# Causal attention with row maxima: diagonal tiles copied by ScalarE, masked by a GpSimd select and reduced from SBUF, in place of mask matmuls

## The reference, cut to what matters

```
att = jnp.einsum('bhqd,bhkd->bhqk', q, k) * scale
att = att + alibi[None]
att = att + causal[None, None]          # -inf above the diagonal
att = jax.nn.softmax(att.astype(jnp.float32), axis=-1)
y = jnp.einsum('bhqk,bhkd->bhqd', att, v)
```

## Time and profile before

| | |
|---|---|
| Time, three runs | 551.94, 554.82, 554.70 us; median 554.7 us |
| The profiled execution | 557.83 us, of which the span of the trace is 556.1 us |
| Busy: PE, DVE, ACT, POOL | 514.5, 298.9, 229.1, 177.5 us |
| Projections with unit 0's row maxima | to 50.7 us |
| Steps 0 to 7 | 57.8 to 274.8 us |
| The rest (output projection, routing, experts, norms) | 274.8 us to the end |

### The profile page before, as it was taken

How to read it: one execution, slowest core, us unless ns; L and a number is a source line. 1 busy time by engine, 2 the same in 40 slices (tenths; PEclk the granted TensorE clock), 3 DMA queues, 4 the chain that set the end, 5 groups by cost and what they waited for, 6 DMA issues and landing times.

```text
span 556.1 us, 7466 instructions
## 1 busy us (share of the span) xinstructions
PE 514.5 (93%) x2538; PEld 256.4 (46%) x2538; DVE 298.9 (54%) x624; ACT 229.1 (41%) x465; POOL 177.5 (32%) x247
## 2 busy tenths in 40 slices
PE   5987999999999999988889899989999999999991
PEld 2432333333333333321166655555656666566661
DVE  1789888888888888860075451211213333334241
ACT  3441676767676767678601131101112222322220
POOL 4432223322222222222100109730022554545543
PEclk9999999999999999999977989999999999999997
DMA  7772455545453545071328100320121221222210
GB/s 225 134 194 73 78 170 89 159 89 175 86 180 87 179 82 183 20 239 47 101 66 285 44 0 1 132 76 20 57 85 49 66 76 59 68 76 57 66 48 28
DMA packets 36868, 54.92 MB, mean 99 GB/s; under 512 B 5647, under 2 KB 24931, under 8 KB 36724
## 3 DMA queue, kind: packets, MB, share of 16 engines
q1 hardware_dynamic: 29792, 30.96, 21.3%
q0 software_dynamic: 7040, 23.50, 13.5%
HBM read 34.76 MB, written 17.52 MB: 94 GB/s over the span
## 4 chain that ended last, share of the span: by engine, by line
PE 81%; DVE 10%; ACT 4%; issue 2%; DMA 1%; POOL 1%; POOLq 0%; SPq 0%; ACTq 0%; DVEq 0%
PE ps L728 14%; PE ps L548 11%; PE ps L523 10%; PE ps L648 10%; PE ps L537 9%; DVE mx L879 7%; PE ps L747 7%; PE ps L659 5%; PE ps L493 3%; PE ps L620 3%; PE ps L739 2%; ACT probs L807 2%; PE ps L525 2%; PE ps L637 1%; PE ps L610 1%
## 5 line engine op out<-in xcount | busy, mean ns | idle before, releaser
L879 DVE TENSOR_REDUCE mx<-ps 128x1 f32<-128x512 f32 (+4 forms) x312 | 183.0, 643 | 29.0 <-PE ps L525 20.9
L807 ACT ACTIVATE probs<-ps 128x512 f32<-128x512 f32 x288 | 151.1, 606 | 68.6 <-PE ps L537 68.6
L523 PE MATMUL ps<-qk_or_dn 127*128 127x512 bf16 (+3 forms) x384 | 117.4, 331 | 5.5 <-DVE mx L879 3.9
L537 PE MATMUL ps<-qk_or_dn 127*128 127x512 bf16 x288 | 100.5, 380 | 2.9 <-ACT probs L807 2.6
L1155 POOL TENSOR_SCALAR_AFFINE_SELECT probs<-probs 128x512 f32<-128x512 f32 x64 | 40.5, 633 | 164.5 <-ACT probs L807 164.5
L728 PE MATMUL ps<-wgu,tmp 128*128 x184 | 82.9, 593 | 0.1
L548 PE MATMUL ps<-probs,Vs 128*32 128x512 f32 x576 | 76.7, 605 | 0.7 <-ACT probs L807 0.7
L523 PEld LDWEIGHTS ps<-qk_or_dn 127*128 127x128 bf16 x384 | 37.1, 97 | 80.1 <-DVE mx L879 63.7
L1203 POOL DMA_INDIRECT rows<-acc,tok x23 | 22.7, 986 | 89.9 <-DMA acc<-x_all 45.1
L1068 DVE TENSOR_TENSOR tmp<-tmp,ps 128x512 f32<-128x512 f32 x23 | 15.8, 688 | 65.0 <-PE ps L728 65.0
L525 PE MATMUL ps<-cb 128*128 128x128 bf16 x256 | 50.6, 222 | 0.0
(11 more groups left out here) (121 smaller groups left out, 470.9 us busy)
## 6 DMA issues: line engine op xcount, KB each, us to landing
wgu<-in_gu POOLq DMA_DIRECT2D x8, 1024.0 KB, 6.1
qk_or_dn<-qparts SPq DMA_DIRECT2D x36, 128.0 KB
yT<-yU SPq DMA_DIRECT2D x16, 256.0 KB, 2.1
qk_or_dn<-in_dn SPq DMA_DIRECT2D x8, 512.0 KB, 8.0
tmp<-xs SPq DMA_DIRECT2D x23, 128.5 KB
qparts<-wgu SPq DMA_DIRECT2D x6, 384.0 KB, 3.3
tmp<-yT SPq DMA_DIRECT2D x34, 64.0 KB
xs<-rows POOLq DMA_DIRECT2D x1, 2056.0 KB, 10.2
```

The costliest lines, as they stand in the source:

```text
L523: mm = pe.matmul(o, q, K6[k][0:KROWS, k0:k0 + w], start=True, stop=not masked)
L537: pe.matmul(o, K6[k][0:KROWS, kb * P:(kb + 1) * P], Q6[k][0:KROWS, :, qi * P:(qi + 1) * P], start=True, stop=True).then_inc(s_st, 1)
L807: act.activation(probs[:, 4 * (s % 3) + p, :], ps[:, 4 + (4 * s + p) % SB, :], ACT.Exp, scale=SCALE).then_inc(s_exp, 1)
L879: dve.tensor_reduce(o, ps[:, a_bank(u, t), 0:nh * w].rearrange("p (h w) -> p h w", h=nh), AX.X, ALU.max).then_inc(s_amax, 1)
```

## The change

A unit's row-max tiles are cut anew. The diagonal block of each `qi` is a tile of its own: 4 heads of 128 keys in one bank, 8 such tiles for a unit. What lies beside the diagonal makes 30 tiles. The mask matmuls and their constant are gone. A diagonal tile goes another way: ACT copies the bank to SBUF (`copy_diag`, two buffers `dg`), POOL fills the part above the diagonal with -3e38 (`cut_diag`), and DVE reduces it from SBUF, four places later in the stream than its own place (`BEHIND`). Its bank is freed by ACT's copy. A unit has 39 places now.

The parts of `split_max` are laid between the first four reductions of the next stream, with one more maximum (`join_max`) ahead of them; the transposition stands at place 6 instead of 3. Each step takes the stream 20 places ahead instead of 15, 14 places run before step 0, step 0 takes 45 and step 6 takes 20. The maxima of a unit are written with one transfer instead of three. POOL's later loads are issued one group later in a step.

```diff
 def row_max_tiles():
-    tiles = []
+    beside = []
+    for qi in range(1, NQ):
+        w = min(qi, 4) * P
+        per = 4 * P // w if w != 3 * P else 1
+        beside += [(qi, h, per, 0, w, LEFT) for h in range(0, HG, per)]
+        if qi > 4:
+            w = (qi - 4) * P
+            per = 4 * P // w if w != 3 * P else 1
+            beside += [(qi, h, per, 4 * P, w, RIGHT) for h in range(0, HG, per)]
+    tiles, n = [], len(beside) - 1
     for qi in range(NQ):
-        w = min(qi + 1, 4) * P
...
+        tiles.append((qi, 0, HG, qi * P, P, DIAG))
+        tiles += beside[n * qi // NQ:n * (qi + 1) // NQ]
+    return tiles + beside[n:]
...
+LEAD, AHEAD, FIRST_AHEAD = 6, 20, 14
+BEHIND, ND = 4, 2
+SPLITS = 4
-LEAD, AHEAD = 3, 15
-ORDER = (SHORT, LONG) * 4 + (SHORT,)
+ORDER = (SHORT, LONG) * 4 + ("SMSMSMWS",)
+def unit_tiles(u):
+
+    tiles = max_stream(u + 1)[AHEAD if u else FIRST_AHEAD:] if u + 1 < NU else []
+    return tiles + (max_stream(u + 2)[:AHEAD] if u + 2 < NU else [])
+def unit_order(u):
+    return (LONG,) * GROUPS if u == 0 else ORDER
+def reduce_order(u):
+
+    own, late = max_stream(u), []
+    out = []
+    for at, (v, t) in enumerate(own):
+        if is_diag(t):
+            late.append((at + BEHIND, (v, t)))
+        else:
+            out.append((v, t))
+        while late and late[0][0] <= at:
+            out.append(late.pop(0)[1])
+    assert not late
+    return out
...
-                for p in range(3):
-                    sp.dma_start(Q6[i][p:p + 1, :, :].rearrange("o h t -> o (h t)")
-                                 .rearrange("o (a b) -> o a b", a=n),
-                                 mrow[p * n:(p + 1) * n, :]).then_inc(s_mrow, 16)
+                sp.dma_start(Q6[i][0:M_ROWS, :, :].rearrange("p h t -> p (h t)")
+                             .rearrange("p (a b) -> p a b", a=HG * NQ), mrow[:]).then_inc(s_mrow, 16)
...
                 if i >= 3:
-                    pe.wait_ge(s_amax, i - 2)
+                    beside, diag = freed(i - 3)
+                    if FREED_BY_ACT[i - 3]:
+                        pe.wait_ge(s_dcopy, diag)
+                    else:
+                        pe.wait_ge(s_amax, beside)
...
-                    masked = diag < w
-                    mm = pe.matmul(o, q, K6[k][0:KROWS, k0:k0 + w], start=True, stop=not masked)
-                    if masked:
-                        mm = pe.matmul(o[:, diag:diag + P], id16, mask_qk, start=False, stop=True)
+                    mm = pe.matmul(ps[:, bank, i * w:(i + 1) * w], Q6[k][0:KROWS, h0 + i, qi * P:(qi + 1) * P],
+                                   K6[k][0:KROWS, k0:k0 + w], start=True, stop=True)
...
+            def copy_diag(u, t, bank):
+
+                n = NQ * u + A_TILES[t][0]
+                act.wait_ge(s_aps, max_index(u, t) + 1)
+                if n >= ND:
+                    act.wait_ge(s_dmax, n - (ND - 1))
+                act.activation(dg[A_TILES[t][0] % ND], ps[:, bank, :], ACT.Copy).then_inc(s_dcopy, 1)
...
-                qi, h0, nh, k0, w, second = A_TILES[t]
+                qi, h0, nh, k0, w, kind = A_TILES[t]
+                if kind == DIAG:
+                    dve.wait_ge(s_dcut, NQ * u + qi + 1)
+                    dve.tensor_reduce(mxd[:, :, qi], dg[qi % ND].rearrange("p (h w) -> p h w", h=HG), AX.X, ALU.max
+                                      ).then_inc(s_dmax, 1)
+                    return
...
+            def join_max(u):
+
+                dve.wait_ge(s_amax, freed(max_index(u, NA - 2))[0])
+                dve.tensor_tensor(mx0[:, :, 5:NQ], mx0[:, :, 5:NQ], mx1[:], ALU.max).then_inc(s_split, 1)
+                dve.wait_ge(s_split, u * 5 + 1)
+                dve.wait_ge(s_dmax, (u + 1) * NQ)
+                dve.tensor_tensor(mxs, mx0[:], mxd, ALU.max).then_inc(s_split, 1)
...
+            def cut_diag(u, t):
+
+                n = NQ * u + A_TILES[t][0]
+                pool.wait_ge(s_dcopy, n + 1)
+                tile = dg[n % ND].rearrange("p (h w) -> p h w", h=HG)
+                pool.affine_select(tile, tile, [[0, HG], [-1, P]], ALU.is_ge, least, base=0, channel_multiplier=1
+                                   ).then_inc(s_dcut, 1)
```

186 lines of the change are left out of this document (114 added, 72 removed).

## The result

The changed kernel takes 558.9 us (median of 10 executions, 556.1 to 560.7), the kernel before 554.6 us (10 executions, 551.9 to 555.5). The ratio of the executions is 1.009 with a 95% interval of 1.007 to 1.011 (the two medians alone would give 1.008): slower, and outside the forecast range of 540.5 to 551.0. The profiled execution took 559.95 us, its span is 558.2.

What follows compares the result with a forecast made beforehand. PE's queue was taken to bound steps 1 to 5, DVE the start. Terms +1.0 (through step 0), -9.7 (steps 1-5), -1.3 (step 6) sum to -10.0 us: 544.7 from median 554.7, stated as 545.0, range 540.5 to 551.0.

Steps and rivals of the forecast that it cites:

- I take +1.5 us (0 to +3): Start, beside the projections: late diagonal reductions make DVE wait for PE's tiles at about four of eight job boundaries; +1.5 us.
- first scores at +0.3: First scores after the start: transposition waits for three more reductions, about 1.5 us, the single transfer returns 1.2; +0.3 us.
- Step 0 itself, -0.8: Step 0: 45 places instead of 40 but no 32 masks, 9.2 us of work instead of 10.1; -0.8 us taken.
- The transposition now comes earlier, so I cost this at nothing: Single transfer of a unit's maxima: lands before the next unit's first score, covered by a full group; no cost.
- 26.0 us a step: Steps 1 to 5: PE's floor of 25.83 us plus 0.2 for waits, instead of 27.94; -9.7 us over five steps.
- the 1.84 written: Steps 1 to 5: 32 mask matmuls of a unit leave PE's queue at 0.0575 us each; -1.84 us a step.
- I take -1.3 us: Step 6: 16 masks (-0.9) and six places go, groups run at ACT's pace, the unspread split is two operations longer; -1.3 us.
- DVE as the bound: Rival, chance 0.16: late diagonal tiles and full banks add 1 us to DVE's 24.0, step 27.0 us, time 550.
- The slower rival: Rival, chance 0.08: DVE waits for each diagonal tile, eight a step; 0.7 us each gives 562, 1.0 about 572.
- ACT's copies against scores: Rival "nothing gained", chance 0.08: copies between exponentials delay PE by 0.23 us each, cancelling 1.84 us; 553 to 556.
- The clock rival: Rival, chance 0.06: the low clock lies over step 0's first groups, 3.5 us at half speed, up to 3 us; 548.
- The port between DVE and POOL: Rival, chance 0.04: selects hold back four two-operand SBUF operations at a unit's boundary, up to 0.63 us each; 547.5.

Runs made afterwards that it cites:

- e5: Changed kernel without the detour: DVE reduces diagonal tiles straight from PSUM, no ACT copies, POOL selects or causal mask in the row maxima; ratio to before 0.992.
- e6: Changed kernel with ACT's copies of unit 0's diagonal tiles ahead of the next job's first copy; ratio to the kernel before 1.006.
- e8: Changed kernel with the edits of e1, e6 and e7 together, and POOL's loads at groups 4 and 7 (4 and 8 in step 0); ratio to before 0.996.
- e9: e8 with the expert slots cleared at the end of step 6 (s == 8) instead of s == 4; 546.8 us, ratio to the kernel before 0.985.
- e10: e8 with the last transposition back in the change's place, slots cleared at s == 4; ratio to the kernel before 0.990.
- e13: e9 with the slots cleared at the start of step 6 (s == 1); median 546.1 us against 554.6 before, ratio 0.984.
- e7: Changed kernel with the last unit's transposition six places later in step 6; ratio to the kernel before 1.014.
- e12: Changed kernel with e7's late transposition, e8's loads and e9's clearing, the start left as the change has it; ratio to before 0.999.
- e2: Changed kernel with POOL's second load of a step one group later (groups 4 and 7 instead of 4 and 6); ratio to the kernel before 1.004.
- e3: Changed kernel with three transfers for the maxima, as before the change; ratio to the kernel before 1.012.
- e11: Kernel before with the second 1 MB load of a step moved to its maxima's transfer (s == 7 instead of 5); ratio to before 1.020.
- e4: Kernel before without its mask matmuls, row maxima over the whole diagonal block; ratio to before 0.987, a step 26.86 us.
- e1: Changed kernel with DVE's reductions beside the projections dealt out by job, never asking for the next job's tile; ratio to before 1.006.

## Why the prediction was wrong

**"I take +1.5 us (0 to +3)" for the start.** This step failed most. Up to the end of step 0 the forecast was +1.0 us and +11.1 came: +6.7 at unit 0's last reduction, where +1.5 was taken, +0.5 to the first scores and +3.9 in step 0. It counted what DVE's queue loses by asking for a tile of the next job, and never laid ACT's queue beside it. There the copy that frees PE's bank stands behind up to three operations of a projection job, one of which waits for DVE. The runs show it: without the detour the maxima of unit 0 come 4.2 to 6.8 us earlier (e5); moving the copies halves DVE's waits for PE (e6); both edits of order bring them from 58.7 to 62.2 us down to 55.0 to 56.0 (e8, e9, e10, e13).

The same code also varied: unit 0's maxima came at 61.4, 62.2 and 61.3 us (after, e7, e12) and at 58.9 and 58.7 (e2, e3). The traces show where most of that arises. A window within the ring and DVE's longest wait for PE near it, first of the changed kernel, then of e2:
```profile
30.00:36.00 6.00, 4.38 (x13) 1.90 (x13) 1.75 (x3) 2.11 (x4) 2.35 (x3) 0.72 0.72 176
36.44 0.69 DVE L958 TENSOR_REDUCE mx<-ps 128x1 f32<-128x512 f32 x1 [3.11 <-PE ps L575]
```
```profile
30.00:36.00 6.00, 3.98 (x19) 1.66 (x20) 3.29 (x6) 2.07 (x5) 1.59 (x3) 1.00 0.77 211
34.00 0.69 DVE L958 TENSOR_REDUCE mx<-ps 128x1 f32<-128x512 f32 x1 [1.42 <-PE ps L575]
```
Where the clock falls to 1.2 GHz inside the ring (a projection's matmul takes 1.16 us at 32.20 and took 0.59 at 24.71), the same wait is 3.1 us and not 1.4. e7 has it at the same place, e12 between 44 and 53 us (0.62 granted, a wait of 3.09 us); in e2 and e3 the clock stays at 1.00 up to 53 us. That is 1.7 of the 2.5 us between after and e2; the other 0.8 stand there already at DVE's first reduction that waits for PE (22.50 for 21.74). So a part of the miss at the start is a low clock in the changed kernel's profile that the prediction did not have either.

The next step, first scores at +0.3, was right at its core: the maxima are copied 4.1 us behind the last reduction instead of 2.6, and from the first issue to the first score it is 3.4 us instead of 4.4, so the single transfer gives 1.0 back and not 1.2 (first scores at 65.00, 57.81 before: +7.2, of which 6.7 were there at the last reduction). Step 0 itself, -0.8, was wrong by 4.7 us: from the first scores to its end it takes 34.25 us where 30.31 did before. The low clock (2.1 us) and the wait for the maxima of unit 1, behind the load of 88.54 (1.3 us), make 3.4 of them; the rest isn't placed. In e8, e12 and e13, which don't have that wait and have the low clock some 3 us long there, it takes 32.2 us.

**"The transposition now comes earlier, so I cost this at nothing. Its cover is a full group."** Cover against what came 1.8 us after the issue. I named PE's work behind the transfer and not the queue ahead of it: the diff moves POOL's loads from groups 3 and 5 to 4 and 6, and a 1 MB load ahead of a 24 KB transfer makes 3.3 us into 6.2. e2 (taken away), e3 (number of transfers ruled out) and e11 (made in the kernel before) show it from three sides. The 1.8 us were also the wrong row for the single transfer, which takes 3.3 us with nothing ahead of it. In steps 1 to 5 it is worth 0.5 us each (26.58 to 26.08).

**"26.0 us a step", -9.7.** Right in size once the loads are moved: 26.04 to 26.24 in e2, e8 to e10, e12 and e13. The terms under it were half right. The masks alone give 1.08 us and not the 1.84 written, since DVE at 23.8 us then delays the transposition (e4). The other 0.8 us came with the new stream, the spread split and the detour, where the prediction had the transposition's 0.42 less 0.15 for the finer tiles; which of them gives how much isn't shown, but without the detour the step stays at 26.5 (e5). The floor "25.83" was a tenth or two too low. DVE busy 23.75, ACT 23.50 and POOL 14.36 are the forecast 24.0, 23.6 and 14.0.

**Step 6, "I take -1.3 us": +1.7.** The split in a row was put at two small operations, some 0.4 us. PE stood 3.15 us instead of 1.2: DVE still had 1.15 us of reductions when PE had nothing more to do, where before a weighing of 1.07 us stood, and the split took 0.8 us more and not 0.4. Two of its operations took 0.40 and 0.50 us instead of 0.17 and 0.18, the second inside a select of POOL (245.48 to 246.16). The low clock behind the hole took about another 0.5 us: e1 and e3 have the same hole of 3.15 us, a full clock behind it, and 27.66 and 27.54 us for the step (with 1.2 and 1.0 us of waiting for the last maxima in it), where the changed kernel has 28.14. The true room was larger than forecast, too: with the transposition late and the transfer free, step 6 takes 23.63 us, 2.8 less than before (e9, e12, e13). I had the room at 1.3 because I counted the groups' pace and left the hole of before in.

**The rivals.** DVE as the bound: no; in steps 1 to 5 it waited for PE and never for a select. The slower rival placed the loss at DVE's wait for a diagonal tile; the sign was its, the mechanism wasn't. ACT's copies against scores cost nothing in the steps, where only 1.9 us of PE's waits in five steps were for maxima and 0.6 for `kparts` (Q and K's load, also costed at nothing). The clock rival came true in part: the low clock lay over step 0's first groups at the price it named (2.1 us where it said up to 3), on top of the rest. It isn't the detour's alone, since e5 and e13 have it from 50 to 61 us too, where DVE is the bound. It is more than the prediction's one place: the mean granted clock is 0.953 to 0.962 in the ten executions of the changed kernel, 0.972 in the profiled one before, and 0.967 to 0.980 in before's executions beside the experiments.

*The port between DVE and POOL* was there, and small. Two of DVE's small operations of the changed kernel, and POOL's select next to each:
```profile
57.43 0.47 DVE L994 TENSOR_TENSOR mx<-mx 128x12 f32<-128x12 f32 x1
...
60.24 0.18 DVE L1010 TENSOR_TENSOR mparts<-mrest,mparts 128x32 bf16<-128x32 f32 x1
```
```profile
57.24 0.63 POOL L1206 TENSOR_SCALAR_AFFINE_SELECT dg<-dg 128x512 f32<-128x512 f32 x1
...
60.30 0.63 POOL L1206 TENSOR_SCALAR_AFFINE_SELECT dg<-dg 128x512 f32<-128x512 f32 x1 [2.42 <-ACT dg L834]
```
The first starts inside a select and ends with it, 0.47 us instead of 0.17; the second starts 0.06 us ahead of a select and takes its 0.18. One or two such hits a unit, some 0.2 to 0.4 us each, did not reach DVE's bound in steps 1 to 5; in step 6, where PE waits for the split, a hit is a part of the hole. And it is not "only those four operations" that pay: L1003, a `tensor_scalar` that reads one tensor, took 0.50 us at 245.70 inside a select. By the rule of the Trainium skill, SBUF — State Buffer, "Who interferes with whom", the engine that comes first holds the shared ports for its whole instruction; the trace agrees, and reductions from SBUF stayed at 676 ns, as it says.

## What to carry to other kernels

When an operation moves to another in-order queue, write out for each stage what stands ahead of it there and what that waits for; the steady steps, where the queues had room, came near the sum, and the start, where one engine was full, lost more than all of them won. When a diff moves a large load by one group, lay the small transfers that someone waits for beside it: here the second 1 MB load of each step, in the wrong group, cost the kernel before 2.0% (e11) and the changed one, whose loads met the transfer as well, some 0.5 us a step (e2), and one collision after another came up each time the one ahead was mended (loads, then the slots' clearing against the last maxima, then against the denominators). Mend such faults together before you judge a change: alone, three of the four edits gave 0.3 to 0.5% and one made it slower, together they turned 1.009 into 0.996, and with the clearing of the slots moved as well into 0.985.
